# Flamingo block with gated attention and a routed expert layer: the last two chunks' up weights copied in SBUF, and a new order of all engines

## The chip, the core and the metric

The kernel runs on one NeuronCore of a Trainium2 chip. A core has five engines with a queue each: TensorE (matrix products, in the profile PE, its weight loads PEld), VectorE (DVE), ScalarE (ACT), GpSimd (POOL) and SyncE (SP), which only issues transfers here. Engines wait for each other by semaphores and run their own queues in order. All transfers share 16 DMA engines. The metric is the device time in microseconds; the time before is the median of three runs.

## The reference

The input x has 128 sequences of 64 tokens with 128 numbers each; in all 8192 tokens. Two sublayers follow each other, each behind a layernorm and added with a gate:

```python
scores = jnp.einsum('bsqd,bskd->bsqk', qh, kh) / math.sqrt(hd)   # 16 x 16 heads within one token
...
x = x + jnp.tanh(g_xattn[0]) * _L0_xattn_ref(_layernorm(x), ctx_1024, ctx_1024)
...
logits = xf @ router_w.T + experts_bias
rw, sel = jax.lax.top_k(logits, K)                               # 2 of 8 experts
eo = jax.nn.silu(g) * u                                          # g, u: 128 -> 256, per expert
moe_out = jnp.einsum('te,teh,ehd->td', cw, eo, w2)
x = x + jnp.tanh(g_ffn[0]) * (moe_out + shared_out)
```

The attention is among the 16 heads of a single token, causal over the heads, so it is elementwise work. The expert layer takes for each token two of eight experts (up weights 128 x 512 for gate and value together, down weights 256 x 128) and one shared expert that every token passes.

## The kernel before

**Chunks.** The tokens go in nine chunks of 4, 8, ..., 8, 4 tiles of 128 tokens. For each chunk VectorE makes the attention's products (`qk`, lines 768 and 773 for scores; `pv`, line 800; `add`, line 808), TensorE sums the `pv` products (`SUM`), and VectorE makes the residual (`att`, `x1`). Then the router: `turn` and `logit` on TensorE, `top`, `pos` and `tab` on VectorE. `tab` writes a table (line 916) that says for each block of 128 routed rows which expert it belongs to and where it lies.

**Scatter and blocks.** GpSimd scatters the normalised tokens into `rows_in` in DRAM, sorted by expert (`scatter`, line 680). SyncE reads them back in blocks of 128 rows. For a block, `block_in` reads the table into a register (line 546), loads that expert's up weights, 256 KB, into one of eight buffers `wq` (line 549), and loads the rows with 65 KB into one of 16 buffers `xr` (line 558). At the end of three sets of chunks (chunks 0 to 3, 4 to 7, and 8) SyncE first clears the rows behind the last filled ones (`zero`, line 566, eight transfers). There are 149 blocks; those of chunks 7 and 8 are the last 45, numbers 104 to 148.

**Units.** Two blocks of a chunk make a pair; there are 76 pairs, 53 to 75 of them for chunks 7 and 8. A pair is turned by TensorE (`tr`, line 1164), copied by ScalarE (`xrT`, line 1075), multiplied by the up weights (`upR`, line 1193), goes through `sil` on ScalarE (line 1068) and the product `eo` on VectorE (line 939), and through the down weights (`down`, line 1226). ScalarE evacuates and scales it (`yr`, line 1089), and GpSimd scatters it into `ybuf` in DRAM (`post`, line 688), one transfer for each block. The shared expert has 32 units (`upS`, line 1178, two tiles each) with the same `sil`, `eo` and `down`, whose results go to `xo`. So there are 108 units with an up and a down each; TensorE keeps two of them open (two PSUM buffers `ps_g`).

**The way out.** For chunks 0 to 5 GpSimd adds the two scattered results into `xo` by accumulating transfers (`acc`, line 705), each of which waits for the one before it. For chunks 6 to 8 SyncE loads both results back into the buffer of the `pv` products once the set's scatters have landed (`back`, line 574), and VectorE adds them (`mix`, lines 952 and 957, two of each per half of a chunk). `result` stores `xo` (line 581).

**The order.** Nothing is interleaved by hand. The function `planned` plays the kernel through with an estimated duration for each step (`put`) and picks at each moment the step with the lowest urgency `URG` among those that could start within `AHEAD` of the earliest. The resulting list of each engine is then written out as its program. A block was counted there as 1.75 us of SyncE, more than the issue takes, in the place of its transfer.

## Time and profile before

| | |
|---|---|
| median of 3 runs | 623.38 us (622.37 to 626.16) |
| the profiled execution | 626.74 us, span 625.0 us |
| busy of the span: PE, DVE, ACT, POOL | 74%, 76%, 55%, 60% |
| TensorE's granted clock, mean | 0.909 of full speed |
| moved by DMA | 96.23 MB, 154 GB/s |
| loads of up weights | 149 of 256 KB |

The profile is of one execution. A line begins with its start and its duration in us, then the engine, the line of the code, the operation and `out<-in`; in brackets stands the idle time ahead of it and what ended it. SPq is SyncE's queue with its issues. The shares of busy time are means over a first part in which VectorE has most work and a last one in which TensorE has, so they are read by stage.

### The profile page before, as it was taken

What the parts mean: (1) busy time and instruction counts of PE and PEld (TensorE: products, weight loads), DVE (VectorE), ACT (ScalarE), POOL (GpSimd) and SP (SyncE); (2) the same over time, 40 slices, a digit from 0 to 9 for tenths busy, and PEclk for the clock granted to TensorE, in tenths of its full rate; (3) what the DMA queues carried; (4) which work ended last, traced back from release to release, by engine and by line L of the source; (5) the groups of instructions that cost most, each with busy time, mean ns of one, the idle gap of its engine ahead of it and who ended that gap; (6) DMA issues with size and microseconds to landing.
All of it is one profiled execution on the core that took longest, in us unless ns stands there. A gap on an engine that the chain in (4) does not pass through costs nothing.

```text
span 625.0 us, 11721 instructions
## 1 busy us (share of the span) xinstructions
PE 464.2 (74%) x3090; PEld 398.1 (64%) x3090; DVE 473.8 (76%) x991; ACT 345.5 (55%) x1106; POOL 377.3 (60%) x370
## 2 busy tenths in 40 slices
PE   0256736861899789979987899687959899888840
PEld 0144425630778677868787878575758889878840
DVE  4998997999899898999996889969958535221132
ACT  5317529908846784898275886852247354344320
POOL 2102461286167767777887578868846777745742
PEclk9995985995699989999998999988979999999985
DMA  6401112034445672476457632991886657577894
GB/s 239 124 9 58 39 35 71 1 77 151 150 130 159 179 207 82 145 209 178 128 180 218 201 98 88 227 267 43 182 248 193 180 180 213 168 224 217 226 268 166
DMA packets 68848, 96.23 MB, mean 154 GB/s; under 512 B 11256, under 2 KB 39048, under 8 KB 68784
## 3 DMA queue, kind: packets, MB, share of 16 engines
q1 hardware_dynamic: 57040, 69.88, 38.1%
q0 software_dynamic: 11456, 25.59, 15.4%
q8 instruction: 28, 0.46, 0.3%
q14 instruction: 36, 0.29, 0.2%
q10 hardware_dynamic: 288, 0.00, 0.0%
HBM read 69.30 MB, written 26.71 MB: 154 GB/s over the span
## 4 chain that ended last, share of the span: by engine, by line
PE 26%; DVE 18%; POOL 18%; ACT 14%; issue 11%; DMA 9%; SPq 3%; POOLq 0%; DVEq 0%; ACTq 0%
POOL rows_in L680 12%; PE ps_g L1193 11%; PE ps_y L1226 6%; DVE prod L768 5%; ACT xn L999 5%; DVE sc L773 4%; PE ps_g L1178 4%; POOL ybuf L688 3%; DMA ybuf<-yr,xr 3%; DVE pv L800 3%; DMA pv<-ybuf 2%; DMA xr<-rows_in 2%; DVE eo L939 2%; PE ps_o L1132 2%; ACT junk L1020 1%
## 5 line engine op out<-in xcount | busy, mean ns | idle before, releaser
L688 POOL DMA_INDIRECT ybuf<-yr,xr x149 | 160.3, 1076 | 69.1 <-issue 40.3
L680 POOL DMA_INDIRECT rows_in<-xn,idx x128 | 157.8, 1233 | 39.5 <-issue 39.2
L1193 PE MATMUL ps_g<-xrT,wq 128*128 128x128 f32 x1192 | 156.0, 287 | 9.1 <-ACT xrT L1075 8.0
L1193 PEld LDWEIGHTS ps_g<-xrT,wq 128*128 128x128 f32 x1192 | 148.2, 202 | 14.6 <-ACT xrT L1075 12.1
L939 DVE TENSOR_TENSOR eo<-sil,ps_g 128x512 f32<-128x512 f32 (+1 forms) x108 | 72.2, 674 | 92.9 <-ACT sil L1068 84.5
L1226 PE MATMUL ps_y<-w2s,eo 128*128 (+1 forms) x852 | 119.5, 284 | 30.5 <-DVE eo L939 20.2
L1226 PEld LDWEIGHTS ps_y<-w2s,eo 128*128 128x128 f32 x852 | 107.2, 195 | 45.5 <-issue 37.9
L1068 ACT ACTIVATE sil<-ps_g 128x512 f32<-128x512 f32 (+1 forms) x108 | 63.5, 589 | 72.9 <-PE ps_g L1193 57.9
L768 DVE TENSOR_TENSOR prod<-xn,ct 128x512 f32<-128x512 f32 (+21 forms) x144 | 93.6, 651 | 5.9 <-ACT xn L999 5.9
L773 DVE TENSOR_REDUCE sc<-prod 128x64 f32<-128x512 f32 (+21 forms) x144 | 92.7, 648 | 0.0
L800 DVE TENSOR_TENSOR pv<-ex,ct 128x512 f32<-128x512 f32 (+21 forms) x144 | 88.9, 652 | 1.8 <-PE ps_o L1132 1.6
L1132 PE MATMUL ps_o<-pv,ident 128*128 128x512 f32 (+5 forms) x232 | 75.4, 453 | 3.5 <-DVE pv L800 3.5
L655 POOL TENSOR_TENSOR rstd<-ve,mhalf 128x8 f32<-128x8 f32 (+1 forms) x18 | 29.5, 1638 | 70.9 <-ACT ve L1024 67.3
L1089 ACT ACTIVATE yr<-ps_y,xr 128x128 f32<-128x128 f32 x149 | 46.8, 366 | 43.2 <-PE ps_y L1226 37.0
L1178 PE MATMUL ps_g<-xnT,ws 128*128 128x256 f32 x256 | 66.6, 410 | 0.0
L1075 ACT COPY xrT<-ps_r 128x256 f32<-128x256 f32 (+1 forms) x76 | 27.6, 364 | 67.9 <-PE ps_r L1164 61.7
L999 ACT ACTIVATE xn<-x,shift,rstd 128x128 f32<-128x128 f32 x128 | 53.0, 486 | 8.4 <-POOL shift L658 8.4
L1132 PEld LDWEIGHTS ps_o<-pv,ident 128*128 128x128 f32 x232 | 41.3, 196 | 23.4 <-issue 11.3
L1178 PEld LDWEIGHTS ps_g<-xnT,ws 128*128 128x128 f32 x256 | 51.0, 209 | 6.9
L1164 PE MATMUL ps_r<-ident,xr 128*128 128x128 f32 x149 | 32.1, 288 | 23.3 <-DMA xr<-rows_in 22.3
L1130 PE MATMUL ps_o<-pv,ident 128*128 128x256 f32 (+11 forms) x88 | 29.7, 422 | 23.6 <-DVE pv L800 21.4
L1010 ACT ACTIVATE junk<-x 128x128 bf16<-128x128 f32 x52 | 15.3, 298 | 49.3 <-DVE x L834 49.2
(106 smaller groups left out, 516.0 us busy)
## 6 DMA issues: line engine op xcount, KB each, us to landing
wq<-wall SPq DMA_DIRECT2D x149, 256.0 KB
xr<-rows_in SPq DMA_DIRECT2D x149, 65.0 KB, 3.1
xo<-ybuf POOLq DMA_DIRECT2D x10, 512.0 KB
xt<-in_x SPq DMA_DIRECT2D x7, 512.0 KB, 3.9
ct<-in_ctx SPq DMA_DIRECT2D x7, 512.0 KB, 4.9
out<-xo SPq DMA_DIRECT2D x7, 512.0 KB, 4.5
xo<-x POOLq DMA_DIRECT2D x5, 512.0 KB, 6.5
ybuf<-yr,xr POOLq DMA_INDIRECT x149
```

Of the source, the lines that this page charges most:

```text
L680: pool.indirect_dma_start(rows_in, bass.IndirectOffsetOnAxis(ap=idx[:, c % 2, k, t:t + 1], axis=0), xn2[:, c % XN, k, t], None).then_inc(s ...
L688: pool.indirect_dma_start(ybuf, bass.IndirectOffsetOnAxis(ap=xr_i[:, BLOCK[c, r + a] % XG, D + 1:DW], axis=0), yr[:, i % YR, a], None, bou ...
L768: nc.vector.tensor_tensor(tiled(diag(prod, PR, m, g), n), xn1[:, 0:n, g * HD:], ch[:, :, 0:WIDTH[g]], ALU.mult).then_inc(s["qk"], 1)
L773: nc.vector.tensor_reduce(sc[:, 0:n, g - 1:NH, g - 1], paired(diag(prod, PR, m, g - 1), n), X, ALU.add).then_inc(s["score"], 1)
L800: nc.vector.tensor_tensor(paired(diag(pv, PV, m, g), n), ex[:, 0:n, g:NH, g].unsqueeze(3).broadcast_to([P, n, NH - g, HD]), by_head(ch)[:, ...
L939: nc.vector.tensor_tensor(eo[:, n % 2, :, 0:w], sil[:, n % 2, :, 0:w], ps_g[n % 2][:, 1, :, 0:w], ALU.mult).then_inc(s["eo"], 1)
L999: nc.scalar.activation(dst[:, t], src[:, c % 2, t], ACT.Identity, bias=shift[w][:, c % 2, t:t + 1], scale=rstd[w][:, c % 2, t:t + 1]).then ...
L1068: nc.scalar.activation(sil[:, n % 2, :, 0:w], ps_g[n % 2][:, 0, :, 0:w], ACT.Silu).then_inc(s["sil"], 1)
L1132: last = nc.tensor.matmul(OUT[:, 1, 0:TILE[m], max(g * HD - HALF_D, 0):], ident[:], products[:, :, split:], start=(g == 0), stop=(g == SUM ...
L1178: last = nc.tensor.matmul(ps_g[n % 2][:, q // HC, q % HC], ws[:, q * P:(q + 1) * P], xnT[:, c % XT, t:t + 2], start=True, stop=True)
L1193: last = nc.tensor.matmul(ps_g[n % 2][:, q // HC, q % HC, a * P:(a + 1) * P], wq[:, b % WR, q * P:(q + 1) * P], xrT[:, i % 3, a * P:(a + 1 ...
L1226: last = nc.tensor.matmul(ps_y[:, a * D:(a + 1) * D], eo[:, n % 2, c, a * P:(a + 1) * P], w[:, c * D:(c + 1) * D], start=(c == 0), stop=(c ...
```

## The change

For blocks of chunks 7 and 8 SyncE no longer loads up weights block by block. When the last chunk's scores and differences are through (their buffers `prod` and `sc` now lie in one tensor `work`, and are needed no more), it loads the up weights of all eight experts once, 2 MB, into `work`. VectorE then reads the table into a register for each of the 45 blocks and copies 128 x 512 numbers out of `work` into the buffer `wq`, and TensorE waits for that copy instead of a transfer.

The plan changes with it. A block costs SyncE 1.0 us there, 0.6 from block 104 on; each transfer is now also counted in a common queue (`CARRIED`, `moved`), and the steps that wait for it come later if the queue is full; all weights `URG` and `AHEAD` are new. So the order of every engine is another from its beginning on.

```diff
+    COPIED = {BLOCK[x] for x in BLOCK if x[0] >= CHUNKS - 2}
+    FROM = min(COPIED)
...
-        URG = {('sp', 'load'): 2.4, ('sp', 'result'): 0.3, ('sp', 'block'): -2.1, ('sp', 'zero'): 5.5,
+        URG = {('sp', 'load'): 2.1, ('sp', 'result'): -0.5, ('sp', 'block'): 3.8, ('sp', 'zero'): 5.2,
...
+        CARRIED = {'load': 0.39, 'block': 1.16, 'result': 0.21, 'acc': 0.3, 'res': 0.3, 'back': 0.39, 'zero': 2.15, 'scatter': 0.73, 'post': 0.37}
+        moved = [0.]
...
-            put("sp", "block", ("block", b), 1.75,
+            put("sp", "block", ("block", b), 1.0 if b < FROM else .6 + 1. * (b == FROM),
...
-                (waits(("upR", RPAIR[BLOCKS[b - WR]])) if b >= WR else []) +
+                (waits(("upR", RPAIR[BLOCKS[b - WR]])) if WR <= b < FROM else []) + (waits(("sub", CHUNKS - 1, 1)) if b == FROM else []) +
...
+            if b >= FROM:
+                put("dve", "copy", ("copy", b), .75,
+                    waits(("tab", c, TABLE), ("upR", RPAIR[BLOCKS[b - WR]])) + [(("block", FROM), 12.)])
...
+            if key[0] in CARRIED:
+                cost = CARRIED[key[0]]
...
+                ends[key] += max(0., moved[0] - at - dur)
+                moved[0] = max(moved[0], at + dur) + cost
...
-        prod = sb("prod", [P, PR, T * D])
+        work = sb("work", [P, PR * T * D + T * NH * NH])
+        prod = work[:, 0:PR * T * D].rearrange("p (b w) -> p b w", b=PR)
+        up_w = work[:, 0:(E + 1) * 2 * H].rearrange("p (e h) -> p e h", e=E + 1)
...
+                if b == FROM:
+                    sp.wait_ge(s["score"], NH * CHUNKS)
+                    sp.wait_ge(s["sub"], 2 * CHUNKS)
+                    sp.dma_start(up_w[:, 0:E], wall[0:E].rearrange("e p h -> p e h")).then_inc(s["up_w"], 16)
...
+            def copy(b):
+                c, r = BLOCKS[b]
+                if b == FROM:
+                    dve.wait_ge(s["up_w"], 16)
+                if r == 0:
+                    dve.wait_ge(s["tab"], c + 1)
+                at = dve.value_load(table[r:r + 1, c:c + 1], min_val=0, max_val=E * SPAN - 1)
+                dve.wait_ge(s["gu"], PLACE["R", RPAIR[BLOCKS[b - WR]]] + 1)
+                nc.vector.tensor_copy(wq[:, b % WR], up_w[:, bass.ds(at >> 7, 1)].rearrange("p e h -> p (e h)"))\
+                    .then_inc(s["copied"], 1)
...
-                    pe.wait_ge(s_wq[b % WR], 16 * (b // WR + 1))
+                    need(pe, *((s["copied"], b - FROM + 1) if b >= FROM else (s_wq[b % WR], 16 * (b // WR + 1))))
```

Three places show what the new order does. In the rows below a name is `out<-in`; line numbers after the change are some 27 to 40 higher.

**TensorE, pairs 72 and 73 near the end.** A turn is the row with `ps_r`, an up the row with `ps_g`, a down those with `ps_y`. Before:

```order
L1164 MATMUL ps_r<-ident,xr 128x128 x2
L1193 MATMUL ps_g0<-xrT,wq 128x128 x8
L1205 TENSOR_LOAD table
...
L1226 MATMUL ps_y<-w2s,eo 128x128
...
L1164 MATMUL ps_r<-ident,xr 128x128 x2
L1193 MATMUL ps_g1<-xrT,wq 128x128 x8
```

After:

```order
L1233 MATMUL ps_g0<-xrT,wq 128x128 x8
L1245 TENSOR_LOAD table
...
L1204 MATMUL ps_r<-ident,xr 128x128 x2
L1266 ISA
L1266 MATMUL ps_y<-w2s,eo 128x128
...
L1233 MATMUL ps_g1<-xrT,wq 128x128 x8
```

Before, a pair's turn stands right ahead of its own up; now a down lies between a turn and the next up, and the turn is that of a later pair.

**VectorE's and GpSimd's last rows.** On VectorE the products are the rows `eo`, the mixes the rows `pv<-pv` and `xo<-xo,pv`; the last product has one block (128x2x128). Before:

```order
L939 TENSOR_TENSOR eo<-sil,ps_g 128x512 x15
L952 TENSOR_TENSOR pv<-pv 128x512
L957 TENSOR_TENSOR xo<-xo,pv 128x512
L939 TENSOR_TENSOR eo<-sil,ps_g 128x2x128
L952 TENSOR_TENSOR pv<-pv 128x512
```

After, from the last copies on:

```order
L975 TENSOR_LOAD table
L975 ISA x2
L977 ISA
L977 COPY wq<-work 128x512
L966 TENSOR_TENSOR eo<-sil,ps_g 128x512 x3
L990 TENSOR_TENSOR pv<-pv 128x512
L995 TENSOR_TENSOR xo<-xo,pv 128x512
...
L966 TENSOR_TENSOR eo<-sil,ps_g 128x512
L990 TENSOR_TENSOR pv<-pv 128x512
...
L966 TENSOR_TENSOR eo<-sil,ps_g 128x2x128
```

Half a chunk's mix stood ahead of the last product; now a whole chunk's mix stands ahead of the product before the last, and another ahead of the last. On GpSimd, with the scatters as `ybuf` and the accumulations as `xo<-ybuf`, before:

```order
L688 DMA ybuf<-yr,xr 16512x128 x34
L705 DMA xo<-ybuf 128x1024
L688 DMA ybuf<-yr,xr 16512x128 x4
L705 DMA xo<-ybuf 128x1024 x2
L688 DMA ybuf<-yr,xr 16512x128 x4
L705 DMA xo<-ybuf 128x1024
L688 DMA ybuf<-yr,xr 16512x128 x5
```

After:

```order
L715 DMA ybuf<-yr,xr 16512x128 x38
L732 DMA xo<-ybuf 128x1024
L715 DMA ybuf<-yr,xr 16512x128 x4
L732 DMA xo<-ybuf 128x1024 x2
L715 DMA ybuf<-yr,xr 16512x128 x9
L732 DMA xo<-ybuf 128x1024
```

The last accumulation moved from ahead of the last five scatters to behind them.

**SyncE around zero.1, the clearing behind chunk 7.** Its rows are `rows_in<-empty`, one of eight shown. Before, the clearing follows a store and goes ahead of block 104:

```order
L581 DMA out<-xo 128x1024
L565 TENSOR_LOAD rest
L565 ISA x2
L566 ISA
L566 DMA rows_in<-empty 128x130
...
L546 TENSOR_LOAD table
L546 ISA x2
L549 ISA
L549 DMA wq<-wall 128x512
```

After, eight blocks of chunk 6 come between, of which the last is shown, and then the load of all experts:

```order
L592 TENSOR_LOAD rest
L592 ISA x2
L593 ISA
L593 DMA rows_in<-empty 128x130
...
L576 DMA wq<-wall 128x512
L585 ISA
L585 DMA xr<-rows_in 128x130
L571 DMA work<-wall 128x8x512
L572 TENSOR_LOAD table
```

Blocks 96 to 103, which stood ahead of the clearing, moved behind it, and the new load stands behind those.

## Rows read from the trace of the kernel before

**Rows 1.** Busy us (and instructions) by stage: PE, PEld, DVE, ACT, POOL; PE clock, DMA share, GB/s.
```profile
25.00:491.88 466.88, 364.40 (x2298) 305.07 (x2299) 418.52 (x853) 287.33 (x938) 292.88 (x264) 0.90 0.48 136
...
550.00:575.00 25.00, 21.77 (x181) 20.10 (x180) 4.80 (x7) 10.55 (x28) 12.05 (x13) 1.00 0.78 223
575.00:600.00 25.00, 22.18 (x184) 20.57 (x184) 4.80 (x7) 10.76 (x29) 16.61 (x17) 1.00 0.86 227
```

**Rows 2.** Timeline of PE at 520 us: up, turn, down, up.
```profile
520.72 1.95 PE L1193 MATMUL ps_g<-xrT,wq 128*128 128x128 f32 x16
522.51 0.38 PE L1164 MATMUL ps_r<-ident,xr 128*128 128x128 f32 x2
522.73 1.06 PE L1226 MATMUL ps_y<-w2s,eo 128*128 x8
523.62 1.95 PE L1193 MATMUL ps_g<-xrT,wq 128*128 128x128 f32 x16
```

**Rows 3.** Chain of waits from 555 us: start, us, what.
```profile
555.36 2.05 PE ps_g L1193 x16
...
558.56 0.38 ACT xrT L1075
558.94 0.04 issue
558.99 2.05 PE ps_g L1193 x16
```

**Rows 4.** Timeline of SyncE's issues at 549 us.
```profile
549.45 0.33 SPq L549 DMA_DIRECT2D wq<-wall  x1
549.98 0.33 SPq L558 DMA_DIRECT2D xr<-rows_in  x1
551.11 0.33 SPq L549 DMA_DIRECT2D wq<-wall  x1
```

**Rows 5.** Timeline of the end, from the first loads back on.
```profile
591.63 1.85 SPq L574 DMA_DIRECT2D pv<-ybuf  x4
...
604.77 0.69 DVE L952 TENSOR_TENSOR pv<-pv 128x512 f32<-128x512 f32 x1 [5.78 <-DMA pv<-ybuf]
605.54 0.95 POOL L705 DMA_DIRECT2D xo<-ybuf  x1 [6.72 <-DMA xo<-ybuf]
...
606.76 1.22 PE L1226 MATMUL ps_y<-w2s,eo 128*128 x4 [6.30 <-DVE eo L939]
...
608.02 0.37 ACT L1089 ACTIVATE yr<-ps_y,xr 128x128 f32<-128x128 f32 x1 [6.90 <-PE ps_y L1226]
...
613.03 0.98 POOL L688 DMA_INDIRECT ybuf<-yr,xr  x1 [0.31 <-issue]
617.55 0.80 SPq L574 DMA_DIRECT2D pv<-ybuf  x2
...
622.58 0.34 SPq L581 DMA_DIRECT2D out<-xo  x1
```

**Rows 6.** Timeline of PE: the last sums of the last chunk.
```profile
490.13 1.25 PE L1132 MATMUL ps_o<-pv,ident 128*128 128x160 f32 x10
```

**Rows 7.** VectorE's only copies within SBUF: ns min/median/max, first and last start.
```profile
L929 DVE COPY cur<-front x3: 155/172/217, 261.8 to 521.0; 128x8 f32<-128x8 f32 x3
```

**Rows 8.** Timeline of SyncE at zero.1: eight clearings, block 104's weights, its rows.
```profile
488.73 8.04 SPq L566 DMA_DIRECT2D rows_in<-empty  x8
497.64 0.52 SPq L549 DMA_DIRECT2D wq<-wall  x1
501.65 0.35 SPq L558 DMA_DIRECT2D xr<-rows_in  x1
```

**Rows 9.** Timeline of GpSimd's scatters, and VectorE's work on `pv` meanwhile (busy, count).
```profile
424.52 0.97 POOL L680 DMA_INDIRECT rows_in<-xn,idx  x1 [0.30 <-issue]
425.80 1.41 POOL L680 DMA_INDIRECT rows_in<-xn,idx  x1 [0.30 <-issue]
...
434.92 1.63 POOL L680 DMA_INDIRECT rows_in<-xn,idx  x1 [0.30 <-issue]
...
425.80:436.55 10.75, 9.34 (x11) 0.84 0.11 33
```

More of the change, by code:

```diff
@@ L112, in gated_attention_moe @@
     URGENT = (0, 1, CHUNKS - 2, CHUNKS - 1)
+    COPIED = {BLOCK[x] for x in BLOCK if x[0] >= CHUNKS - 2}
+    FROM = min(COPIED)
+    assert COPIED == set(range(FROM, len(BLOCKS)))
     def planned():
-        URG = {('sp', 'load'): 2.4, ('sp', 'result'): 0.3, ('sp', 'block'): -2.1, ('sp', 'zero'): 5.5,
-               ('sp', 'back'): -0.5, ('dve', 'ln1a'): 3.4, ('dve', 'scores'): 14.7, ('dve', 'values'): 6.3,
-               ('dve', 'sum'): -0.0, ('dve', 'chain'): 0.3, ('dve', 'slow'): 0.1, ('dve', 'eo'): 4.1,
-               ('dve', 'xo'): 0.8, ('dve', 'mix'): 10.6, ('dve', 'tab'): 11.3, ('pool', 'inv1'): 1.2,
-               ('pool', 'inv2'): 5.6, ('pool', 'scatter'): 3.8, ('pool', 'post'): 14.7,
-               ('pool', 'gather'): 11.7, ('act', 'nsum'): 12.9, ('act', 'scaled'): 3.0,
-               ('pool', 'residual'): -2.3, ('act', 'ln1b'): 11.4, ('act', 'exp'): 5.7, ('act', 'chain'): 7.5,
-               ('act', 'again'): 16.3, ('act', 'sil'): 4.7, ('act', 'xrT'): -3.0, ('act', 'yr'): 2.9,
-               ('pe', 'sums'): 2.7, ('pe', 'chain'): -1.4, ('pe', 'turn'): -0.8, ('pe', 'upR'): 5.2,
-               ('pe', 'upS'): 8.4, ('pe', 'down'): 3.4}
@@ L125, in planned @@
-        AHEAD = {'tr': 0, 'sil': 0, 'eo': 0, 'upR': 1.5, 'inv2': 0.8, 'scatter': 1.5, 'down': 0.2,
-                 'upS': 0.4, 'scores': 0.4, 'gather': 0, 'block': 0.8, 'chain': 0.2, 'turn': 0.4,
-                 'post': 0.8, 'back': 3.0, 'exp': 0.4, 'ln1b': 0.8, 'sums': 0, 'inv1': 3.0, 'sum': 0,
-                 'ln1a': 0.2, 'residual': 0.2, 'result': 0.2, 'values': 0.2, 'tab': 0, 'slow': 0.2,
-                 'xrT': 0.8}
+        URG = {('sp', 'load'): 2.1, ('sp', 'result'): -0.5, ('sp', 'block'): 3.8, ('sp', 'zero'): 5.2,
+               ('sp', 'back'): -0.2, ('dve', 'ln1a'): 4.2, ('dve', 'scores'): 19.9, ('dve', 'values'): 3.7,
+               ('dve', 'sum'): 7.1, ('dve', 'chain'): 1.0, ('dve', 'slow'): -5.7, ('dve', 'eo'): 0.9,
+               ('dve', 'xo'): 1.4, ('dve', 'copy'): 3.5, ('dve', 'mix'): 0.9, ('dve', 'tab'): -1.1,
+               ('pool', 'inv1'): -0.8, ('pool', 'inv2'): 2.6, ('pool', 'scatter'): 2.6,
+               ('pool', 'post'): 6.5, ('pool', 'gather'): -0.8, ('act', 'nsum'): 9.0, ('act', 'scaled'): 4.7,
+               ('pool', 'residual'): 8.7, ('act', 'ln1b'): 2.8, ('act', 'exp'): 8.4, ('act', 'chain'): 6.5,
+               ('act', 'again'): 6.8, ('act', 'sil'): -7.1, ('act', 'xrT'): 2.6, ('act', 'yr'): 5.7,
+               ('pe', 'sums'): 7.1, ('pe', 'chain'): 7.7, ('pe', 'turn'): -12.0, ('pe', 'upR'): 7.7,
+               ('pe', 'upS'): 10.2, ('pe', 'down'): 3.8}
@@ L130, in planned @@
+        AHEAD = {'tr': 0.2, 'sil': 0.8, 'eo': 0.2, 'upR': 0.2, 'inv2': 3.0, 'scatter': 1.5, 'down': 0,
+                 'upS': 0, 'scores': 0.8, 'gather': 0.2, 'block': 0.8, 'chain': 0.4, 'turn': 0.2,
+                 'post': 1.5, 'back': 0, 'exp': 0.8, 'ln1b': 0.2, 'sums': 0, 'inv1': 0.2, 'sum': 0.4,
+                 'ln1a': 0.8, 'residual': 1.5, 'result': 0.2, 'values': 0, 'tab': 0, 'copy': 0, 'slow': 0,
+                 'xrT': 0.2}
         HOP = .15
@@ L978, in _ @@
                     tab(*unit[1:])
+                elif unit[0] == "copy":
+                    copy(unit[1])
                 elif unit[0] == "mix":
```

19 lines of the change are left out of this document (13 added, 6 removed).

## The prediction

> **What bounds the kernel now.** I read the table of busy time by stage first, then the chain of waits, then the timeline at the places where the chain changes engine. Until the attention of the last chunk is done, at 491.9 us, VectorE sets the pace: 418.5 of 466.9 us busy [rows 1]. From there TensorE does: of the last two full stretches of 25 us it is busy for 22 each, VectorE for 5 [rows 1]. TensorE's clock is at its higher level, 2.4 GHz, through those stretches (1.00 granted), so nothing is to be had from it.
>
> In that tail a pair of routed blocks comes at two rhythms. Around 520 us the order is up, turn, down, and the next up starts 523.62 - 520.72 = 2.90 us later, without idle time [rows 2]. From 545 us on the order is up, down, turn, up. Each up then waits for ScalarE's copy of the turned rows: the chain goes through up, down, turn and the 0.38 us of that copy, and the period is 558.99 - 555.36 = 3.63 us [rows 3]. It repeats 13 times, from the up at 548.11 to that at 595.31. Behind it stand two resources that would not carry 2.90 us: SyncE issues a block each 551.11 - 549.45 = 1.66 us, so a pair each 3.3 us [rows 4], and the DMA engines are busy to 0.78 and 0.86 of the stretch [rows 1]; the same bytes in 2.90 instead of 3.63 us would be 0.98 to 1.08 of it. So the slow rhythm is an order of TensorE, but the loads of weights would have forbidden the fast one.
>
> The end is a third stage [rows 5]. The last down starts at 606.76, after 6.30 us of TensorE's idle time, because on VectorE the last product stands behind the first mix, which waits until 604.77 for the loads back issued at 591.63. GpSimd meanwhile is held at an accumulating transfer until 605.54 (6.72 us idle), with five scatters behind it; the last goes out at 613.03. Then follow the last load back (617.55), the last mix and the last store (622.58); the span ends at 625.0.
>
> **What the change does to each stage.** All sums are of the profiled execution: span 625.0 us, its own time 626.74, so 1.74 us lie outside the span. That execution is 3.4 us above the median of the three runs, 623.38, and I take that off at the end.
>
> *Until the last sums.* No operation is removed or added here; only orders differ. VectorE has 466.9 - 418.5 = 48.4 us of idle time in it [rows 1], which a new order could at best reduce and could also add to. Counting in the two orders, VectorE has 74 products of the expert work ahead of the last chunk's residual, 75 before; TensorE has 46 routed pairs and 28 shared units up ahead of its last sum, 49 and 26 before. I take no gain and no loss, and 10 us to either side, a fifth of that idle time. The last sum then ends at 490.13 + 1.25 = 491.4 us as now [rows 6].
>
> *TensorE from there.* After its last sum 34 ups are left (30 pairs, the last of one block, and 4 shared units; 33 before). In the new order the turn of a pair stands one or two ups ahead, so that ScalarE's copy lies under an up or a down, as in the fast rhythm. At 2.90 us each, 1.5 for the single block and 2.0 for the router of the last chunk (its turns, logits and ranks): 33 x 2.90 + 1.5 + 2.0 = 99.2 us. That needs three covers. SyncE: without the weight load a block's issue shrinks by 549.98 - 549.45 = 0.53 us to 1.13, so 2.3 us per pair [rows 4]. DMA: 45 loads of 256 KB go, one of 2 MB comes. VectorE: below.
>
> *The copies.* 45 copies of 128 x 512, two for each product. No such copy is in the trace: the copy of 128 x 8 takes 0.17 us [rows 7], a two-input operation of 128 x 512 0.69 [rows 5]; I take 0.45, the middle, since the copy streams as many elements but from one source. Ahead of each stands a read of the table into a register, some 0.8 us when it stands in line, as between SyncE's issues at 549.98 + 0.33 and 551.11 [rows 4]. TensorE's queue has the same reads between up and down and shows no gap for them [rows 2], so I count them as running beside VectorE's arithmetic: 0.69 + 2 x 0.8 = 2.3 us per pair, under 2.90. In line behind everything they would be 0.69 + 2 x (0.8 + 0.69) = 3.7, and TensorE would follow: 22 x 0.8 = 17 us lost. Nothing reads them in line so far, so this end only stretches the range.
> The first copies stand behind the last shared products and their outputs, so that the first copied pair waits about 2 us: two table reads and a copy after those.
>
> *The load of all experts.* SyncE issues it after zero.1 and eight blocks of chunk 6. As now zero.1 runs from 488.73 for 8.04 us [rows 8], the blocks take 8 x 1.66 = 13.3: issue at about 510. The nearest transfer is that of the loads back, 2 MB beside others, which took 604.77 - 591.63 = 13.1 us until the mix could start [rows 5]. So it is there at 523 or earlier. TensorE comes to the first copied pair after 11 units and the router: 491.4 + 11 x 2.90 + 2.0 = 525.3. It is covered, by some 2 us or more.
> With these TensorE's last down could start at 491.4 + 99.2 + 2.0 - 0.5 = 592.1 us.
>
> *The mixes.* The new order puts both mixes of chunk 6 ahead of the product before the last, and both of chunk 7 ahead of the last. The loads back are issued after the last scatter of chunk 7, some 12 us ahead of that 592.1 (7 pairs, 20 us, less about 8 for evacuation, two scatters and their landing). They took 13.1 us beside weight loads; without these I take 9. Four operations of 0.69 us stand then ahead of each product, so that the last down comes about 4 us late, at 596 (1 if the loads back take 6 us, 8 if they take 13).
>
> *GpSimd.* Two scatters are 2 x (425.80 - 424.52) = 2.56 us per pair [rows 9], within 2.90. The accumulating transfer that held the last five now stands behind all of them. But two-input streams of VectorE lengthen its scatters: five of them took 436.55 - 425.80 = 10.75 us instead of 6.4 beside 9.34 us of VectorE's products [rows 9], 0.46 us for each us. 45 copies x 0.45 x 0.46 = 9.3 us, of which 22 x 0.34 = 7.5 fit in the slack: 2 us late.
>
> *The end.* From the last down to the end it was 625.0 - 606.76 = 18.2 us [rows 5]. In it the evacuation was done at 608.39, its scatter could have gone some 0.3 later and went at 613.03. Without these 4.3, and with 1 us for three stores that now stand behind the last load back, 14.9. Sum: 596 + 2 + 14.9 = 613 us of span, 614.6 of time, and against the median 611.
>
> **The rivals.**
> *GpSimd is held by the copies.* In the rows scatters beside VectorE's products grow from 0.97 to 1.41 and 1.63 us [rows 9]. With copies at 0.69 us, the upper bound, GpSimd loses 45 x 0.69 x 0.46 = 14.3 us, 6.8 beyond the slack instead of 2: time 616; and if a copy holds each scatter for its whole length, 45 x 0.69 - 7.5 = 23.6, 21 more than the sum: 632. Against it: with short copies there is slack enough. The Trainium skill ("SBUF — State Buffer", section "Who interferes with whom") says that a copy within SBUF may use the two-port modes and then holds the ports shared with GpSimd for its whole length, while a tensor_tensor should not hinder descriptor writing; the trace shows such hindrance by tensor_tensor already, and no run here shows the copy. The same skill ("VectorE: DVE Perf Modes", section "Mode 2×_2P — use both read ports for one tensor") gives fp32 copies two elements per cycle; as an estimate from that page, 0.27 us each, even full holding would be 45 x 0.27 = 12 us, some 3 later than my sum.
>
> *The attention ends later.* Orders that push routing and scatters back make VectorE wait for products, as it does for 48.4 us now [rows 1]. 8 to 10 us lost there go straight through: 619 to 621, no change to speak of. As many won give 601 to 603.
>
> *The load of all experts comes late, and the kernel is slower.* On SyncE it stands behind zero.1, which waits for chunk 7's table, and behind eight blocks that wait for buffers. TensorE has some 2 us of cover. Beyond it each us goes through: with 13 us of lateness beyond the cover the gain is gone, with 20 it is 631. For it: before, the first block behind the zeroing waited 4 us for its rows, from 497.64 to 501.65 [rows 8]. Against it: the blocks moved behind it are of an earlier chunk, whose rows are long written.
>
> *The orders don't reach the fast rhythm*, because the turned rows or the products still come late: then 22 pairs keep up to 0.73 us each, 16 us, and only the end gains: 627, no change.
>
> **How the numbers follow.** Forecast (605 to 617) 0.50; attention earlier, below 605, 0.12; GpSimd held or attention later, 617 to 625, 0.21; slow rhythm kept, 627, 0.08; load late, or the copies in line or holding GpSimd throughout, above 629.6, 0.09. A change of under 1% is about what a measurement of this kernel can't tell from none: faster means below 617.1, slower above 629.6. Faster 0.62, same 0.29, slower 0.09. The range reaches from 600, attention earlier, to 625, and leaves out the slow rhythm, the late load and what an earlier attention would give below 600: 0.2 together.
>
> **What would show it.** In the new trace: ups in the tail 2.90 us apart without idle time ahead; copies of 0.3 to 0.7 us under VectorE's idle time; DMA share below 0.6 in the tail; scatters of 0.97 to 1.3 us; the 2 MB load landed before the first copy's turn; the last down within 2 to 8 us of TensorE's other work; no accumulation ahead of the last scatter. The prediction is wrong if the last sum ends outside 481 to 501 us, if TensorE idles ahead of the first copied pair, or if the period stays above 3.2 us.

## The result, and the profile after

The changed kernel takes 604.1 us (median of 4 runs, 601.0 to 608.4) beside 624.8 for the kernel before on the same chip: ratio 0.966, 95% interval 0.958 to 0.975. Run again later it takes 603.6 (6 runs, 601.8 to 606.0) beside 626.1 for the kernel before, ratio 0.968 (0.963 to 0.972). The profiled span is 602.2 us, 22.8 below the 625.0 of before: 15.5 us of that are gone by the end of the last sum, 7.3 behind it.

The table of busy time by stage, to be set beside [rows 1]: us from and to, then PE, PEld, DVE, ACT, POOL, the clock of TensorE, the DMA share, GB/s.
```profile
25.00:476.62 451.62, 358.42 (x2244) 300.20 (x2245) 412.56 (x855) 284.55 (x926) 286.14 (x261) 0.89 0.48 135
500.00:525.00 25.00, 21.90 (x179) 20.42 (x177) 14.56 (x39) 9.57 (x24) 17.62 (x20) 1.00 0.38 104
525.00:550.00 25.00, 25.00 (x223) 24.86 (x222) 15.38 (x27) 13.00 (x35) 17.09 (x18) 1.00 0.34 90
550.00:575.00 25.00, 25.00 (x225) 24.94 (x225) 12.47 (x23) 12.37 (x33) 16.93 (x17) 1.00 0.50 131
```
From 525 to 575 us TensorE is never idle, and the DMA share is 0.34 and 0.50; the last two full stretches before had 0.78 and 0.86. Until the last chunk's residual VectorE is idle for 451.62 - 412.56 = 39.1 us, 48.4 before, and busy for 412.6 us, 418.5 before: of the 15.3 us between the two ends of this stretch 9.3 are idle time and 6.0 busy time.

The timeline of TensorE: the last sums (with [rows 6]), one period of the tail (with [rows 2, 3]) and the last down (with [rows 5]).
```profile
474.86 0.98 PE L1172 MATMUL ps_o<-pv,ident 128*128 128x128 f32 x8
...
528.01 2.05 PE L1233 MATMUL ps_g<-xrT,wq 128*128 128x128 f32 x16
529.90 0.38 PE L1204 MATMUL ps_r<-ident,xr 128*128 128x128 f32 x2
530.12 1.05 PE L1266 MATMUL ps_y<-w2s,eo 128*128 x8
531.01 2.05 PE L1233 MATMUL ps_g<-xrT,wq 128*128 128x128 f32 x16
...
582.36 0.74 PE L1266 MATMUL ps_y<-w2s,eo 128*128 x4 [1.97 <-DVE eo L966]
```
The last sum ends at 474.86 + 0.98 = 475.8 us (491.4 before). Up follows up after 531.01 - 528.01 = 3.00 us, without idle time; at other places it is 2.90. The last down starts 582.36 - 475.84 = 106.5 us after the last sum, and waits 1.97 us for a product that stands behind the mixes.

VectorE, on the timeline: copies (with [rows 7]), the first mix, the last mix.
```profile
510.49 0.43 DVE L977 COPY wq<-work 128x512 f32 x1 [0.47 <-issue]
...
518.75 0.42 DVE L977 COPY wq<-work 128x512 f32 x1
519.54 0.43 DVE L977 COPY wq<-work 128x512 f32 x1 [0.37 <-issue]
...
527.57 0.70 DVE L977 COPY wq<-work 128x512 f32 x1 [0.40 <-issue]
528.20 0.67 DVE L966 TENSOR_TENSOR eo<-sil,ps_g 128x512 f32<-128x512 f32 x1
528.79 0.42 DVE L977 COPY wq<-work 128x512 f32 x1
...
575.58 0.68 DVE L990 TENSOR_TENSOR pv<-pv 128x512 f32<-128x512 f32 x1
...
597.16 0.42 DVE L990 TENSOR_TENSOR pv<-pv 128x256 f32<-128x256 f32 x1 [14.97 <-DMA pv<-ybuf]
```
And GpSimd's scatters beside them, and its end (with [rows 9, 5]).
```profile
527.05 0.98 POOL L715 DMA_INDIRECT ybuf<-yr,xr  x1 [0.30 <-issue]
528.33 1.00 POOL L715 DMA_INDIRECT ybuf<-yr,xr  x1 [0.30 <-issue]
...
576.58 1.89 POOL L732 DMA_DIRECT2D xo<-ybuf  x2 [2.81 <-DMA ybuf<-yr,xr]
...
589.42 0.98 POOL L715 DMA_INDIRECT ybuf<-yr,xr  x1 [0.31 <-issue]
```
A copy takes 0.42 to 0.43 us where nothing lengthens it. Most scatters stay at 0.97 to 1.03; of the 39 from the first to the last copy six take longer, up to 1.25. The last evacuation is done at 583.50; its scatter goes out at 589.42, 5.6 us after it could have, since GpSimd waited 2.81 us at an accumulating transfer and then had nine scatters to issue.

SyncE's queue: the load of all experts (with [rows 4, 8]), the loads back, the stores.
```profile
489.72 0.40 SPq L571 DMA_DIRECT2D work<-wall  x1
...
566.79 2.25 SPq L601 DMA_DIRECT2D pv<-ybuf  x4
...
591.71 0.87 SPq L601 DMA_DIRECT2D pv<-ybuf  x2
595.82 3.52 SPq L608 DMA_DIRECT2D out<-xo  x4
```
The 2 MB load is issued at 489.72, and the first copy, 20.8 us later, doesn't wait for it. The loads back that the first mix reads take at most 575.58 - 566.79 = 8.8 us, since that mix waits for the product ahead of it and not for them; the last ones need 597.16 - 591.71 = 5.5. From the last down to the end it is 602.2 - 582.36 = 19.8 us.

### The profile page after: what moved, and what is told of

It is laid out like the page before. It is cut to its first block, busy times and chain, and to the rows that moved or that the text cites. A ratio compares the mean times of both kernels' runs of the same rounds, so it can differ in the third digit from the quotient of the medians.

```text
span 602.2 us, 11808 instructions
## 1 busy us (share of the span) xinstructions
PE 458.5 (76%) x3090; PEld 397.2 (66%) x3090; DVE 489.9 (81%) x1036; ACT 346.9 (58%) x1106; POOL 373.3 (62%) x370
## 4 chain that ended last, share of the span: by engine, by line
PE 29%; POOL 20%; DVE 14%; issue 11%; ACT 11%; DMA 7%; SPq 6%; POOLq 0%; DVEq 0%; ACTq 0%
POOL rows_in L707 12%; PE ps_g L1233 10%; PE ps_y L1266 7%; PE ps_g L1218 5%; ACT xn L1039 4%; DMA xr<-rows_in 3%; POOL rstd L682 3%; POOL ybuf L715 3%; DVE work L795 3%; DVE pv L827 3%; PE ps_o L1172 3%; DVE work L800 3%; DMA ybuf<-yr,xr 2%; SPq L572 2%; PE ps_r L1204 2%
## 5 line engine op out<-in xcount | busy, mean ns | idle before, releaser
L707 POOL DMA_INDIRECT rows_in<-xn,idx x128 | 150.8, 1178 | 38.3 <-issue 37.4
L1233 PE MATMUL ps_g<-xrT,wq 128*128 128x128 f32 x1192 | 147.1, 279 | 0.4 <-ACT xrT L1115 0.4
L1233 PEld LDWEIGHTS ps_g<-xrT,wq 128*128 128x128 f32 x1192 | 140.9, 195 | 1.7 <-issue 1.0
L1266 PEld LDWEIGHTS ps_y<-w2s,eo 128*128 128x128 f32 x852 | 109.4, 198 | 42.3 <-issue 38.1
L795 DVE TENSOR_TENSOR work<-xn,ct 128x512 f32<-128x512 f32 (+21 forms) x144 | 93.8, 652 | 9.5 <-ACT xn L1039 5.6
L800 DVE TENSOR_REDUCE work<-work 128x64 f32<-128x512 f32 (+21 forms) x144 | 92.8, 649 | 0.0
L1218 PE MATMUL ps_g<-xnT,ws 128*128 128x256 f32 x256 | 68.7, 421 | 2.3 <-DVE eo L966 2.3
L682 POOL TENSOR_TENSOR rstd<-ve,mhalf 128x8 f32<-128x8 f32 (+1 forms) x18 | 33.0, 1836 | 47.9 <-ACT ve L1064 44.0
L1180 PE MATMUL ps_o<-ident,xn 128*128 128x128 f32 x64 | 14.1, 361 | 43.6 <-ACT xn L1039 43.5
L977 DVE COPY wq<-work 128x512 f32 x45 | 23.8, 529 | 22.9 <-PE ps_g L1233 16.3
```

Of the source, the lines that this page charges most:

```text
L707: pool.indirect_dma_start(rows_in, bass.IndirectOffsetOnAxis(ap=idx[:, c % 2, k, t:t + 1], axis=0), xn2[:, c % XN, k, t], None).then_inc(s ...
L795: nc.vector.tensor_tensor(tiled(diag(prod, PR, m, g), n), xn1[:, 0:n, g * HD:], ch[:, :, 0:WIDTH[g]], ALU.mult).then_inc(s["qk"], 1)
L800: nc.vector.tensor_reduce(sc[:, 0:n, g - 1:NH, g - 1], paired(diag(prod, PR, m, g - 1), n), X, ALU.add).then_inc(s["score"], 1)
L1218: last = nc.tensor.matmul(ps_g[n % 2][:, q // HC, q % HC], ws[:, q * P:(q + 1) * P], xnT[:, c % XT, t:t + 2], start=True, stop=True)
L1233: last = nc.tensor.matmul(ps_g[n % 2][:, q // HC, q % HC, a * P:(a + 1) * P], wq[:, b % WR, q * P:(q + 1) * P], xrT[:, i % 3, a * P:(a + 1 ...
L1266: last = nc.tensor.matmul(ps_y[:, a * D:(a + 1) * D], eo[:, n % 2, c, a * P:(a + 1) * P], w[:, c * D:(c + 1) * D], start=(c == 0), stop=(c ...
```

## The experiments

The table gives the start of the last instruction of the last sums, the ratio to the kernel before with its interval, and the mean time from one product to the next between the products 84 and 104 of VectorE, which lie in the tail (the difference of those two starts, over 20). Beside the kernels after the first two rows the kernel before has medians of 624.7 to 626.1 us. The last sum and the time per pair are of one traced execution each; that of "old tables", "no counting", "one accumulation later" and "each copy twice" was the longest of its kernel (643.4, 650.6, 632.4 and 613.4 us).

| kernel | last sum, us | time, us (runs) | ratio | per pair, us |
|---|---|---|---|---|
| before | 491.1 | 624.8 (4) | 1 | 3.46 |
| changed | 475.6 | 604.1 (4) | 0.966 (0.958 to 0.975) | 3.16 |
| changed, again | 475.5 | 603.6 (6) | 0.968 (0.963 to 0.972) | 3.16 |
| orders without copies | 479.7 | 624.7 (4) | 0.998 (0.993 to 1.004) | 4.24 |
| copies in the old order | 488.2 | 625.4 (4) | 1.001 (0.995 to 1.006) | 3.42 |
| old tables | 510.0 | 638.1 (4) | 1.023 (1.016 to 1.030) | - |
| no counting | 520.5 | 646.8 (4) | 1.036 (1.027 to 1.044) | - |
| one accumulation later | 493.2 | 625.1 (12) | 0.999 (0.996 to 1.002) | - |
| accumulations spread | 480.9 | 619.9 (9) | 0.991 (0.988 to 0.995) | 3.54 |
| accumulations gathered | 480.8 | 609.7 (6) | 0.972 (0.968 to 0.977) | 3.15 |
| each copy twice | 481.3 | 608.8 (4) | 0.974 (0.968 to 0.980) | 3.42 |
| another end | 478.6 | 602.9 (6) | 0.964 (0.959 to 0.970) | 3.16 |

The theory, from the two traces: there are two gains, one in the attention, by the orders, and one in the tail, by the copies, which let TensorE keep a fast rhythm. The first two kernels take the change apart into these halves. From the start of the last sum to the end of the span it is 133.9 us in the kernel before and 126.6 in the changed one, 126.0 there in the second trace; without the copies it is 143.5, and with the copies in the old order 134.0.

**The orders without the copies.**
```diff
-                if b == FROM:
...
-                    sp.dma_start(up_w[:, 0:E], wall[0:E].rearrange("e p h -> p e h")).then_inc(s["up_w"], 16)
...
-                if b < FROM:
+                if True:
...
-                    copy(unit[1])
+                    pass
...
-                    need(pe, *((s["copied"], b - FROM + 1) if b >= FROM else (s_wq[b % WR], 16 * (b // WR + 1))))
+                    pe.wait_ge(s_wq[b % WR], 16 * (b // WR + 1))
```


> The new orders word for word on every engine, but no copy on VectorE and no load of all experts: SyncE loads the weights of all 149 blocks one by one, as in the kernel before. Theory (two separate gains: the orders give 15 us in the attention, the copies carry the fast rhythm of the tail): the last sum ends at 474 to 479 us as in the changed kernel (475.8), but in the tail SyncE's issues (3.3 us per pair) and the transfers set the pace of the last 22 pairs, 0.4 to 0.7 us each more: 8 to 15 us, so a time of 612 to 619 and a DMA share above 0.75. Rival (the orders alone made the whole gain, the copies carry nothing): 602 to 606, a period of 2.9 to 3.0 us in the tail. Which part of the gain the copies hold is the difference to the changed kernel's 604.

Measured: 624.7 us, no gain at all. The last sum is early, at 479.7 (474 to 479 were expected), and the whole of it is lost in the tail. Of TensorE's waits from 500 us on this one is the largest (what waited, for what: us in total, times, longest); the second row is SyncE's only wait from 513 to 600 us.
```profile
PE ps_r L1199 <- DMA xr<-rows_in: 17.0, 14, 3.8
```
```profile
SPq L571 <- PE ps_g L1228: 2.1, 3, 1.0
```
SyncE waits for 2.1 of 87 us. It issues block after block, 39 of them from 518.09 to 588.08 us, so 1.84 us each and 3.7 us per pair, and TensorE waits for the rows that stand behind the weights. The DMA share is 0.77 and 0.71 in the stretches 525 to 575; which of the two holds the rows back more, SyncE's issues or the transfers, wasn't tested. The 4.24 us of the table hold two late rows more (the 3.8 us wait, until 591.97) and the up behind them, which took 3.62 us: TensorE's granted clock was 0.50 of full speed, its lower level, from 591.0 to 597.8. So the fast order can't be had with weight loads; the expectation had the mechanism, and sized it 6 us too small at its upper end.

**The copies in the old order.** The planner is that of the kernel before, tables and costs; behind it the copies are put into VectorE's list.
```diff
+    for b in range(FROM, len(BLOCKS)):
+        i = RPAIR[BLOCKS[b]]
+        behind = ("copy", b - 1) if b > FROM and RPAIR[BLOCKS[b - 1]] == i else ("eo", max(i + 27, 81, PLACE["R", i - 4]))
...
+        ORDER["dve"].insert(ORDER["dve"].index(behind) + 1, ("copy", b))
```


> The orders of the kernel before on every engine, with the copies put into VectorE's list four pairs ahead of their use and one load of all experts at block 104. Theory (TensorE's order up, down, turn, up sets the 3.63 us of the old tail): the last sum ends at 488 to 495 us as before, the rhythm from 545 us on stays at 3.5 to 3.7 us although the DMA share falls below 0.6; a time of 617 to 625. Rival (freeing SyncE and the DMA engines is what makes the tail fast, whatever the order): a period of 2.9 to 3.1 us from 545 us on, and 612 or less.

Measured: 625.4 us, again no gain. Busy time in one stretch, and TensorE's timeline in it:
```profile
550.00:575.00 25.00, 21.77 (x181) 20.11 (x180) 10.85 (x22) 10.56 (x28) 11.98 (x12) 1.00 0.22 60
```
```profile
552.73 2.05 PE L1236 MATMUL ps_g<-xrT,wq 128*128 128x128 f32 x16 [0.46 <-ACT xrT L1118]
554.62 1.06 PE L1269 MATMUL ps_y<-w2s,eo 128*128 x8
555.51 0.38 PE L1207 MATMUL ps_r<-ident,xr 128*128 128x128 f32 x2
```
The DMA share falls from 0.78 [rows 1] to 0.22, and TensorE's busy time is 21.77 us to the hundredth, as before: the turn stands right ahead of its own up, and the next up follows at 556.36, 3.63 us later. This is the theory's case. Neither half gains anything; both together gain 3.3%.

**What in the plan gives the attention's gain.** Two kernels, each with one of the plan's two novelties taken back. The first has the tables `URG` and `AHEAD` of the kernel before, with the new entries for the copies kept.

> All of the change but for the planner's two tables of urgency: those are the old ones (with the copies' own entry kept), while the transfers are still counted. Theory (the new tables made the gain in the attention): the last sum ends at 486 to 497 us, as before within what orders vary; a time of 612 to 622. Rival (counting the transfers made it): the last sum at 472 to 480, a time of 600 to 608.

The second leaves out the count of transfers:
```diff
-            if key[0] in CARRIED:
+            if False:
```


> All of the change but for the count of transfers in the planner; its tables of urgency are the new ones. Theory (the new tables made the gain in the attention, by laying the router's small dependent operations among others): the last sum ends at 472 to 481 us and the time is 600 to 610. Rival (counting the transfers made it): the last sum at 486 to 497, a time of 612 to 622.

Measured: 638.1 and 646.8 us, with the last sums at 510.0 and 520.5. Theory and rival both fall: neither the tables nor the count is good by itself. Each of these plans gives another order, and the attention's end lies anywhere in 45 us by it. What has to be explained is one order against another, not one rule of the plan.

So I looked where VectorE stood longest in the kernel before. The timelines of GpSimd and of VectorE have it:
```profile
459.78 0.98 POOL L705 DMA_DIRECT2D xo<-ybuf  x1 [6.88 <-issue]
```
```profile
464.06 0.69 DVE L939 TENSOR_TENSOR eo<-sil,ps_g 128x512 f32<-128x512 f32 x1 [7.57 <-ACT sil L1068]
```
GpSimd is held at an accumulating transfer, with the scatters of six pairs behind it. SyncE issues a block's rows only at 459.40, after a wait for a scatter to land; TensorE waits 3.04 and 3.50 us for rows, and VectorE 7.57 for the product. In the changed kernel its longest wait for ScalarE ahead of a product, up to 476 us, is 2.3 (3.1 in its second trace), and these waits are 11.2 us in all; before they are 27.6.

The next kernel takes the hold for the cause of TensorE's waits. SyncE's and TensorE's timelines in the kernel before show that it isn't:
```profile
447.25 0.38 SPq L558 DMA_DIRECT2D xr<-rows_in  x1
449.27 0.88 SPq L558 DMA_DIRECT2D xr<-rows_in  x1
```
```profile
455.70 0.30 PE L1164 MATMUL ps_r<-ident,xr 128*128 128x128 f32 x1 [3.04 <-DMA xr<-rows_in]
459.50 0.48 PE L1164 MATMUL ps_r<-ident,xr 128*128 128x128 f32 x1 [3.50 <-DMA xr<-rows_in]
459.77 3.62 PE L1193 MATMUL ps_g<-xrT,wq 128*128 128x128 f32 x16
```
By their semaphores the rows that TensorE waits for are these two, issued before GpSimd's hold began (459.78 - 6.88 = 452.90). TensorE had them 8.5 and 10.2 us after their issue, where 3.1 is the median from issue to landing; the DMA share was 1.01 from 450 to 456. The up behind them, whose product VectorE waits for, took 3.62 us instead of 1.95 [rows 2]: after those two idle stretches the granted clock was 0.50, the lower level, from 457 to 463. So late transfers and then a lower clock stand ahead of the 7.57 us, not the hold.

**One accumulation later**, in the kernel before.
```diff
+    shift("pool", ("acc", 3, 1), ("post", 45))
```


> The kernel before with one unit moved: GpSimd's last accumulating transfer of chunk 3 stands behind the scatters of six more pairs instead of ahead of them. Theory (the new order's gain in the attention is a hold resolved: in the kernel before GpSimd is held 6.88 us at this transfer at 452.9 us, the scatters behind it free no buffer, SyncE's rows come late, TensorE waits 3.04 and 3.50 us for them at 455.7 and 459.5 and VectorE 7.57 us for a product at 464.06): the 7.57 us fall below 2, the last sum ends at 483 to 487 us instead of 491.4, and the time falls by 4 to 8 us. Rival (the gain is spread over many places and other waits move up): the last sum ends at 489 to 493, and the time stays within 2 us.

Measured: ratio 0.999, the last sum at 493.2. Its profiled execution was its longest (630.5 us of span, the median of its times is 625.1), so I take from it only where a wait lies:
```profile
458.62 0.48 DVE L951 SCALAR_TENSOR_TENSOR xo<-ps_y,tg,x 128x256 f32<-128x256 f32 x1 [7.48 <-PE ps_y L1232]
```
VectorE now waits 7.48 us, 5 us earlier and for something else: ScalarE had waited 10.79 us for a scatter to land before it could evacuate. One hold taken away leaves the next. By its time this was the rival's case, and the single hold is not the cause.

**The accumulations spread**, in the kernel before: what both waits have in common is that transfers land late.
```diff
+    shift("pool", ("acc", 1, 1), ("post", 35))
+    shift("pool", ("acc", 2, 0), ("acc", 1, 1))
+    shift("pool", ("acc", 2, 1), ("scatter", 6, 4))
+    shift("pool", ("acc", 3, 0), ("acc", 2, 1))
+    shift("pool", ("acc", 3, 1), ("scatter", 6, 6))
```


> The kernel before with five units of GpSimd moved: the accumulating transfers of chunks 1 to 3 that stood together among the scatters of the pairs 36 to 39 now go out earlier, before and between the scatters of chunk 6's rows, where the changed kernel has them. Theory (in the kernel before the DMA engines are at 0.24 to 0.30 at 420 to 440 us and then at 0.88 to 0.93 until 460, when scatters, accumulations, rows and weights meet; VectorE is busy 5.64 of the 10 us from 450 on): with the accumulations in the idle stretch the share at 440 to 460 falls below 0.8, the wait of 7.57 us goes, the last sum ends at 482 to 487, the time falls by 4 to 8 us. Rival (the attention's gain doesn't hang on these transfers): last sum at 488 to 493, the time within 2 us of the kernel before.

Busy time in two stretches, of the kernel before and then of this one:
```profile
420.00:440.00 20.00, 16.71 (x93) 13.33 (x92) 19.96 (x33) 6.32 (x14) 16.95 (x13) 0.91 0.27 72
440.00:460.00 20.00, 12.54 (x66) 9.59 (x65) 15.57 (x50) 3.39 (x8) 11.20 (x12) 0.92 0.90 222
```
```profile
420.00:440.00 20.00, 14.64 (x84) 11.10 (x83) 17.80 (x29) 4.87 (x10) 15.58 (x14) 1.00 0.64 159
440.00:460.00 20.00, 19.42 (x129) 16.31 (x127) 18.97 (x65) 10.38 (x26) 15.26 (x16) 1.00 0.72 210
```
The DMA share goes from 0.27 and 0.90 to 0.64 and 0.72, VectorE is busy for 18.97 us of the second stretch instead of 15.57, the 7.57 us wait is gone (the longest is 3.0), the last sum comes at 480.9, even ahead of the 482 to 487 that were expected, and the time falls by 0.9%, some 5 us. Theory's case: by these traces, with 491.1 and 488.2 for the old order, the gathered transfers cost its attention 7 to 10 us, of which some 5 show in the time.

**The accumulations gathered**, in the changed kernel, as the counterpart.
```diff
+    shift("pool", ("acc", 1, 1), ("scatter", 6, 7))
+    shift("pool", ("acc", 2, 0), ("acc", 1, 1))
+    shift("pool", ("acc", 2, 1), ("post", 38))
+    shift("pool", ("acc", 3, 0), ("acc", 2, 1))
+    shift("pool", ("acc", 3, 1), ("post", 39))
+    shift("sp", ("result", 1), ("block", 89))
+    shift("sp", ("result", 2), ("block", 93))
+    shift("sp", ("result", 3), ("block", 103))
```


> The changed kernel with those five accumulating transfers put where the kernel before has them, behind the scatters of chunk 6's rows and among those of the pairs 38 to 40, and the three stores that wait for them later on SyncE's queue. Theory (these transfers, gathered there, hold scatters, rows and products): VectorE gets a wait of 4 us or more between 440 and 470 us, the last sum ends at 481 to 486, the time is 4 to 8 us above the changed kernel's 603.6. Rival: last sum at 474 to 480, the time within 2 us of 603.6.

The same stretches:
```profile
420.00:440.00 20.00, 20.00 (x119) 16.79 (x118) 19.45 (x56) 5.90 (x14) 15.06 (x14) 1.00 0.18 52
440.00:460.00 20.00, 13.91 (x73) 11.70 (x73) 13.41 (x48) 12.78 (x29) 8.70 (x10) 0.66 0.91 215
```
The DMA engines show the picture of before again, 0.18 and then 0.91. The last sum comes at 480.8, 5.2 us after that of the changed kernel; but the other three kernels with this order until there have it at 478.6 to 481.3, so this alone says little. VectorE's idle time from 25 us to the end of the last sum is 43.7 us, 39.0 in the changed kernel and 42.0 to 44.3 in those three. The wait of 4 us comes too (4.53 at 473.68), a little later than expected. The time is 609.7, and the intervals of the two ratios overlap. It points the way of the theory and doesn't show it for the new order.

**Each copy twice**, in the changed kernel.
```diff
+                    .then_inc(s["once"], 1)
+                dve.wait_ge(s["once"], b - FROM + 1)
+                nc.vector.tensor_copy(wq[:, b % WR], up_w[:, bass.ds(at >> 7, 1)].rearrange("p e h -> p (e h)"))\
                     .then_inc(s["copied"], 1)
```


> The changed kernel with each of the 45 copies made twice, the second behind the first. Theory (VectorE has the room: 2.95 us per pair with 0.6 us of product and 1.1 us of copies; GpSimd is not held): scatters in the tail stay at 0.98 to 1.1 us, the period rises from 2.95 to at most 3.3 us, the time by 0 to 7 us. Rival (the copies hold GpSimd, or the reads of the table stand in line with them on VectorE, which is then the bound at 3.3 us and more): scatters of 1.3 us and more or a period of 3.5 us and more, the time 12 us longer or worse.

Measured: 608.8 us, 5.2 above the changed kernel on the same chip (by the ratios 3.9). The costliest groups of VectorE have the two copies (count, us in all, mean ns of one, idle time ahead), and TensorE's timeline has the two waits that this costs:
```profile
L977 DVE COPY wq<-work 128x512 f32 x45 | 20.6, 458 | 12.4 <-issue 6.9 <-PE ps_g L1236 5.4
L980 DVE COPY wq<-work 128x512 f32 x45 | 20.5, 455 | 1.5
```
```profile
524.12 1.15 PE L1269 MATMUL ps_y<-w2s,eo 128*128 x8 [1.98 <-DVE eo L966]
...
530.76 2.05 PE L1269 MATMUL ps_y<-w2s,eo 128*128 x8 [2.58 <-DVE eo L966]
```
Twenty more us of VectorE cost 4 to 5, and those where the first copies fill the ring of weight buffers (1.98 + 2.58); the second down takes 2.05 us instead of 1.15, with the granted clock at 0.50 from 531 to 534. From the last sum to the end this trace has 130.3 us, 126.6 in the changed kernel. From 550 to 575 us TensorE is busy throughout, with the up 2.90 us after the up before. GpSimd isn't held: its 41 scatters between the products 84 and 104 take 1.02 us on average, 1.01 in the changed kernel, 0.99 in the kernel before. The 3.42 us per pair of the table, which hold the filling of the ring, lie between the theory's 3.3 and the rival's 3.5; by the scatters, the time and the steady part it is the theory's case: there copies have room for twice their cost.

**Another end**, in the changed kernel.
```diff
+    shift("dve", ("eo", 106), ("eo", 105))
+    shift("dve", ("eo", 107), ("eo", 106))
+    shift("pool", ("acc", 4, 1), ("post", 73))
+    for n, unit in enumerate([("result", 6), ("result", 7), ("back", 8), ("result", 4), ("result", 5)]):
+        shift("sp", unit, ("back", 7) if n == 0 else last)
+        last = unit
```


> The changed kernel with another end: VectorE's last two products stand ahead of all mixes, GpSimd's last accumulating transfer of chunk 4 behind three more pairs' scatters, and SyncE's stores of chunks 6 and 7 ahead of the last load back, those of chunks 4 and 5 behind it. Theory (GpSimd's 2.81 us hold at 576.58 and TensorE's 1.97 us wait for the product behind the mixes delay the last scatter, 589.42, and with it the last load back): the last scatter goes out at 585 to 587, the last mix's load 3 to 4 us earlier, the time 2.5 to 5 us under the changed kernel's. Rival (the last load back waits for the other transfers, not for the scatter): the time within 1 us of the changed kernel's.

Measured: 602.9 us beside 603.6, intervals that overlap: no difference that can be told. That is the rival's number, but it doesn't decide between the two: from the start of the last sum to the end this trace has 123.8 us, 2.2 to 2.8 less than the two of the changed kernel, while its last sum comes 3 us later than theirs, and the last scatter went out at 588.73 instead of 585 to 587. GpSimd's last scatter, TensorE's last down, SyncE's last issues and VectorE's last mix:
```profile
588.73 0.98 POOL L726 DMA_INDIRECT ybuf<-yr,xr  x1 [0.30 <-issue]
```
```profile
582.83 0.71 PE L1277 MATMUL ps_y<-w2s,eo 128*128 x4 [0.94 <-ACT yr L1140]
```
```profile
592.30 0.88 SPq L612 DMA_DIRECT2D pv<-ybuf  x2
593.23 7.13 SPq L619 DMA_DIRECT2D out<-xo  x3
```
```profile
598.18 0.43 DVE L1001 TENSOR_TENSOR pv<-pv 128x256 f32<-128x256 f32 x1 [11.19 <-DMA pv<-ybuf]
```
The hold is gone, but the last scatter still goes out 4.5 us after it could have (the last evacuation is done at 583.95), instead of 5.6: GpSimd issues scatters back to back from 576 on and is the bound there. The last load back is issued 592.30 - 588.73 = 3.6 us after the last scatter (2.3 in the changed kernel), and needs 5.9 us beside the stores (5.5). From the last down to the end it is 19.6 us, 19.8 there.

**The changed kernel again.**

> The changed kernel once more, on the chip of the other three, as their measure. It is expected within 3 us of 604; its last sum between 473 and 480 us.

Measured: 603.6 us, the last sum at 475.5. No version made here beats the changed kernel by more than can be measured.

## Why the prediction was right, and where not

The time lies in the range and the direction is right, but it isn't the case that the text held likeliest (605 to 617, 0.50): it is "attention earlier, below 605", which had 0.12. The point, 611, is 7 us too high, and that error has parts that go against each other. The span fell by 22.8 us where the sum had 12: the last sum came 15.5 us earlier than in the sum, the way from there to the last down took 1.9 us longer, and the end 2.9 longer. To the extent that those two hide the miss in the attention, it is luck that the point is only 7 us off.

*Until the last sums: no gain, 10 us to either side.* This is the step that failed: 15.5 us were gained, and the text had named 481 to 501 as the bounds of being right; it was 475.8. The rival "the attention ends earlier" is what happened. Over the five traces with the new order there the last sum starts at 475.5 to 481.3, on average 478.1; the two with the old order have 491.1 and 488.2, so the order is worth some 11.5 us and the rest is what traces vary by. I had counted products, which indeed hardly moved, and bounded the gain by VectorE's idle time alone.

What the runs showed in its place has two parts. The first is busy time, which the sum held fixed. From 25 us to the end of the last sum VectorE is busy for 418.1 to 418.5 us in the four traces with its old order ("before", "copies in the old order", and the two with accumulations moved in the kernel before), and for 411.7 to 412.4 in the six with its new one. That is 6 us of the 11.5. It goes with the order and not with the accumulating transfers: in the traces of "accumulations spread" (old order) and "accumulations gathered" (new order) the last sum ends at the same time, and VectorE's busy time, the third of the five, differs by 6.0 us:
```profile
25.00:481.22 456.22, 359.40 (x2293) 300.92 (x2294) 418.42 (x852) 287.31 (x939) 289.54 (x262) 0.91 0.49 139
25.00:481.12 456.12, 359.20 (x2237) 302.33 (x2238) 412.41 (x853) 284.93 (x926) 283.21 (x258) 0.89 0.47 133
```
The instructions aren't shorter: their durations add up to 489.9 us before and 489.4 after. They overlap more, small dependent operations of the router above all (the eight rounds of `avail` ahead of the last sum last 1.47 us together and add 0.53 to the busy time; in the old order 1.64 and 1.24). This is read from traces alone, and why they overlap more stays open. The second part is idle time: 39.0 to 44.3 us over those five traces, 48.3 and 45.0 in the two with the old order. There transfers matter: spreading the accumulating ones alone brings the old order's idle time to 37.8 us. That the new order gains by the same is not shown: putting them back there gave nothing that could be told from the spread.

*TensorE from there, 2.90 us per pair with three covers.* Right in mechanism. Without the copies the rows come late behind SyncE's weight loads and the order loses all it won; without the order the copies change nothing. The 0.73 us per pair of the old rhythm went down to nothing (the up after 2.90 to 3.00 us). TensorE's own stretch was 3.9 us longer than the sum: without its last wait the last down would have started 104.6 us after the last sum, where the sum had 100.7 (the 0.5 us that it takes off has no source in it). Waits of 1.06, 0.46, 0.72 and 0.46 us make 2.7 of that. TensorE's idle 1.00 + 0.46 + 0.46 us ahead of the first copied pair's up, at 513.15, fit the 2.0 of the sum, though the text had also named idle time there as a sign of being wrong; the kernel without copies has the same three waits.

*The copies, 0.45 us.* Measured 0.43 alone and 0.53 on average. The 0.27 us worked out in the rival was too short: it counted the elements alone, though a copy of 128 x 8 takes 0.17 already [rows 7]. The reads of the table don't cost 0.8 us nor nothing: 0.37 to 0.67 between two of the first copies, 0.22 at most behind a product. The rival of reads in line had its place but not its price.

*The load of all experts* came 20 us earlier than I had it, because the zeroing that it stands behind had moved with it (467.9 instead of 488.73). The rival by which it came late fell there.

*The mixes, 4 us.* The last down waited 1.97 us behind them and the one before 0.46; the loads back of chunk 6 took at most 8.8 us, 9 predicted.

*GpSimd 2 us late, and the end 14.9.* It was 5.6 us late, and from the last down to the end it is 19.8 us where the sum had 2 + 14.9. I had only moved the accumulation that held the last scatters; another, `acc(4, 1)`, then held five pairs. Nor is that the whole: without it the queue still was 4.5 us behind; 2.56 us of scatters per pair leave little in 2.90 for the accumulations, which stand among them and take 1.0 each. The copies had little part in it: the 9.3 us by which they were to lengthen the scatters came out as 1.2 (1.7 with each copy twice), so the 0.46 us for each us, read beside the `pv` products [rows 9], doesn't hold for copies.

*The rival "GpSimd is held by the copies".* It fell by its price: doubling the copies left its scatters at 1.02 us on average. Of 45 copies 20 took 0.57 us or more, and the longest scatter beside them took 1.25. The Trainium skill ("SBUF — State Buffer", section "Who interferes with whom") calls this an exclusive lock, held for the whole instruction, that the loser waits for. The trace agrees that one is lengthened beside the other, but not for the whole instruction: the wait is 0.28 us at most, on either side, where a scatter takes 0.98 and a copy 0.43.

## What to carry to other kernels

Where two limits lie one under the other (here TensorE's order above SyncE's weight loads), taking away either alone gains nothing, and each of two such tests alone would have called the change useless: test the halves and the whole. Engines that wait in order turn one late transfer into waits elsewhere; before you call a held engine the cause, check that what the waiter needed was issued after the hold began. When a wait vanishes and the time stays, look at when the transfers are issued in the stretch before it, not at the next wait. And what a new order can gain isn't bounded by idle time: the busy time of the same instructions can change too. An order found by a plan's weights is a single point: both neighbours of this one were slower than the kernel before, so time the order itself, and credit no single weight with it.
